# The order of additions and gathers on GpSimd's queue in a 64-expert mixture of experts

## What is computed

```python
x = hidden_states.reshape(-1, H)                       # T = 4096 rows of 512
probs = softmax(x @ gate_w)                            # E = 64 experts
w, idx = top_k(probs, 8)
...
buf = zeros((E, CAPACITY + 1, H)).at[e_flat, slot].set(x[tok])   # CAPACITY = 256 rows an expert
gu_e = einsum('ech,ehf->ecf', buf, expert_gate_up_w)
act = silu(gu_e[..., :I]) * gu_e[..., I:]
out_e = einsum('eci,eih->ech', act, expert_down_w)
y = out_e[e_flat, slot] * w_flat[:, None]              # summed over the 8 experts of a row
```

## Time and profile before

| | us |
|---|---|
| median of three runs | 2777.36 |
| the profiled execution's own time | 2763.05 |
| its span, first to last instruction | 2761.3 |
| TensorE busy (matmul) | 2557.5 (93% of the span) |
| TensorE weight loads busy | 1360.6 (49%) |
| VectorE busy | 1559.4 (56%) |
| ScalarE busy | 1353.8 (49%) |
| GpSimd busy | 1342.8 (49%), of it additions 240.9 and the experts' gathers 157.3 |
| mean granted TensorE clock | 0.97 |

### The profile page before, as it was taken

One profiled execution on the slowest core, in us unless ns is written; L12 is line 12 of the kernel. 1 busy time (PEld: TensorE's weight loads), 2 busy tenths in 40 slices (PEclk: granted clock), 3 DMA queues, 4 the chain that ended last, 5 costly groups with the idle time before them and its releaser, 6 DMA issues. The chain is left out here.

```text
span 2761.3 us, 43744 instructions
## 1 busy us (share of the span) xinstructions
PE 2557.5 (93%) x16510; PEld 1360.6 (49%) x16510; DVE 1559.4 (56%) x2474; ACT 1353.8 (49%) x3019; POOL 1342.8 (49%) x1043
## 2 busy tenths in 40 slices
PE   6888879999999899999999978887999999999999
PEld 4333334444444377777777634443444444444444
DVE  6899976555555255665655568775643332334222
ACT  4878874222222166666666468886433222232221
POOL 4777770665555546676666458886102211121111
PEclk9899999999999999999999989998999999999999
DMA  7899995222221399999999879998410111011000
GB/s 211 164 200 182 187 172 187 62 62 62 62 62 46 88 307 289 284 291 285 287 280 289 183 151 192 199 178 199 133 38 16 47 46 35 12 46 46 24 8 31
DMA packets 638576, 389.77 MB, mean 141 GB/s; under 512 B 472096, under 2 KB 575264, under 8 KB 634400
## 3 DMA queue, kind: packets, MB, share of 16 engines
q1 hardware_dynamic: 601504, 319.65, 45.6%
q0 software_dynamic: 36864, 67.34, 12.0%
HBM read 198.86 MB, written 75.89 MB: 99 GB/s over the span
## 5 line engine op out<-in xcount | busy, mean ns | idle before, releaser
L1765 POOL DMA_INDIRECT ids<-sh_tk,sh_su x256 | 269.2, 1052 | 243.0 <-PE sh_gu L55 69.5
L2714 POOL TENSOR_TENSOR fe_prodT<-fe_pp,fe_prodT 128x512 f16<-128x512 f32 x64 | 77.8, 1215 | 590.9 <-ACT fe_prodT L2499 590.9
L55 PE MATMUL ex_gu<-ex_xT,ex_h 128*128 128x256 f16 x3072 | 347.5, 273 | 2.8 <-issue 2.0
L2166 POOL DMA_INDIRECT xp<-ex_oo,ex_to x128 | 240.9, 1882 | 178.1 <-ACT ex_oo L2074 140.6
L55 PEld LDWEIGHTS ex_gu<-ex_xT,ex_h 128*128 128x128 f16 x3072 | 301.3, 98 | 51.9 <-issue 2.1
L1901 DVE SCALAR_TENSOR_TENSOR ex_h<-ring,ex_h 128x1024 f16<-128x1024 f32 x128 | 151.1, 1222 | 158.3 <-ACT ex_h L1891 158.3
L55 PE MATMUL at_g<-hm_zT,hm_w 128*128 128x512 f16 x768 | 187.0, 398 | 14.6 <-DMA hm_zT<-hm_zs 10.9
L2630 DVE SCALAR_TENSOR_TENSOR ring<-fe_g,fe_nf,ring 128x512 f32<-128x512 f32 x32 | 24.0, 751 | 293.1 <-PE fe_g L2415 293.1
L1875 POOL DMA_INDIRECT ex_xg<-zrows,ex_idxu x128 | 157.3, 1229 | 55.5 <-issue 31.1
L55 PE MATMUL sh_g<-sh_wdn,sh_actT 128*128 128x512 f16 x768 | 171.2, 382 | 10.3 <-issue 6.8
L55 PE MATMUL ex_o<-ex_h,ex_aT 128*128 128x512 f16 x768 | 177.9, 382 | 0.2 <-ACT ex_oo L2074 0.2
(11 more groups left out here) (367 smaller groups left out, 5375.7 us busy)
## 6 DMA issues: line engine op xcount, KB each, us to landing
ring<-L_ffn_expert_gate_up_w SPq DMA_DIRECT2D x128, 512.0 KB
ring<-L_ffn_expert_down_w SPq DMA_DIRECT2D x128, 256.0 KB
ring<-x SPq DMA_DIRECT2D x24, 1024.0 KB, 5.9
x<-ring SPq DMA_DIRECT2D x16, 1024.0 KB, 4.8
zrows<-hm_zs SPq DMA_DIRECT2D x32, 256.0 KB
xp<-ring SPq DMA_DIRECT2D x8, 1024.0 KB
out<-ring SPq DMA_DIRECT2D x8, 1024.0 KB, 4.3
ring<-xp SPq DMA_DIRECT2D x7, 1024.0 KB, 6.3
```

What stands on the lines that cost most here:

```text
L55: mm = nc.tensor.matmul(out, lhs(a, k), rhs(b, k), start=start and i == 0 and j == 0, stop=stop and i == n - 1 and j == 2)
L1765: e.indirect_dma_start(ids, bass.IndirectOffsetOnAxis(slotu[b % 2][:, t, j:j + 1], 0), pair[b % 2][:, t, j, :], None, bounds_check=SLOTS - ...
L2166: e.indirect_dma_start(dst, bass.IndirectOffsetOnAxis(to[:, n:n + 1], 0), o32[y % 2][:, t, :], None, bounds_check=T + SLOTS - 1, oob_is_er ...
L2714: e.tensor_tensor(prodT[:, 1, j, :], p32[q % 2][:, :], prodT[:, 0, j, :], ALU.subtract).then_inc(s["p_lo"], 1)
```

## The change

Only GpSimd's list changes. The four indirect DMAs of a round are the same ones with the same waits; their order becomes addition (y, 0), gather (y+5, 0), addition (y, 1), gather (y+5, 1).

```diff
-            for x in range(2, E + AHEAD):
+            def gather(x, t):
+                n = NS * x + t
                 if x < E:
-                    for n in range(NS * x, NS * x + NS):
-                        if n >= NG:
-                            e.wait_ge(s["x_mm"], n - NG + 1)
-                        X.gpsimd_rows(n, zrows)
-                if x >= AHEAD:
-                    y = x - AHEAD
-                    if y:
-                        e.wait_ge(added, 16 * NS * y)
-                    for t in range(NS):
-                        n = NS * y + t
-                        e.wait_ge(s["o_out"], n + 1)
-                        e.indirect_dma_start(dst, bass.IndirectOffsetOnAxis(to[:, n:n + 1], 0), o32[y % 2][:, t, :], None,
-                                             bounds_check=T + SLOTS - 1, oob_is_err=True, compute_op=ALU.add
-                                             ).then_inc(added, 16)
+                    if n >= NG:
+                        e.wait_ge(s["x_mm"], n - NG + 1)
+                    X.gpsimd_rows(n, zrows)
+
+            for x in range(2, AHEAD + 1):
+                for t in range(NS):
+                    gather(x, t)
+            for y in range(E):
+                if y:
+                    e.wait_ge(added, 16 * NS * y)
+                for t in range(NS):
+                    n = NS * y + t
+                    e.wait_ge(s["o_out"], n + 1)
+                    e.indirect_dma_start(dst, bass.IndirectOffsetOnAxis(to[:, n:n + 1], 0), o32[y % 2][:, t, :], None,
+                                         bounds_check=T + SLOTS - 1, oob_is_err=True, compute_op=ALU.add
+                                         ).then_inc(added, 16)
+                    gather(y + AHEAD + 1, t)
```

## The result

The new order took 3061.94 us (median of 5 runs, 3059.12 to 3063.17); the kernel before, run beside it, took 2775.11 us (5 runs, 2759.68 to 2780.97). The ratio is 1.1039, 95% interval 1.1019 to 1.1059. It is slower, as forecast, but by 287 us where 141 were forecast, and the time lies outside the range of 2830 to 2995. The profiled span is 3061.3 us, 300.0 more than before.

What follows compares the result with a forecast made beforehand. GpSimd's loop of landings was taken as the bound; its terms summed to 11.72 us a round, +140.9 us over 59 rounds, 2904 us profiled. With the runs' median 14.3 us higher, the forecast was 2918 us, range 2830 to 2995.

Steps and rivals of the forecast that it cites:

- The bound: Experts' stage: GpSimd's loop from landing to landing, 9.25 us a round, sets the pace; TensorE follows.
- The insertion: GpSimd, between the additions: gather 0 takes 1.62 us, addition 1 2.61; addition 1 ends 2.31 us later.
- Rival 1: GpSimd's round: gather 0 costs only 0.99 us, addition 1 1.57; +33 us, 2810; 8% together with its harsher form.
- harsher form: GpSimd's round: descriptor generation is small, so only the 0.30 us gap is added; +18 us, 2795; within the 8%.
- Covered work: ScalarE, VectorE and TensorE have 2.5 to 3 us of slack a round and cost nothing; rounds 59 to 63 stay.
- the tail: From the end of addition 1 on GpSimd to the next landing: taken as 4.5 us, the unknown term.
- the middle row: The tail of the profiled middle round before the change, 4.34 us, between ends of 3.62 and 6.26.
- argument against: On the tail: a longer round leaves the DMA engines, at 1.07 now, room, countering weights in flight; 4.5 us taken.
- Rival 2: Tail: weights get in addition 1's way, 6.26 us as in round 2; 13.48 us a round, +245 us, 3022; 8%.
- Rivals 3 and 4: Experts' rounds: faster, if TensorE's gather waits bound, 2750 (7%); unchanged, DMA engines alone setting the round, 2777 (5%).

Runs made afterwards that it cites:

- e1: c0 with a pause of three GpSimd memsets between the two additions of rounds 0 to 58, no gather between them; 3002.68 us.
- c1: Order after the change, with attention's DMA transposes replaced by plain copies and 1e-5 added inside one logarithm; 3042.74 us.
- e2: c1 with expert weight loads from expert 3 on cut to 8 of 256 columns, same number of packets; 2842.54 us.
- e4: c1 with full weights, SyncE issuing expert x's loads only once the additions up to expert x-7 have landed; 2856.09 us.
- c0: Order before the change, with attention's DMA transposes replaced by plain copies and 1e-5 added inside one logarithm; 2766.04 us.
- e5: c1 with the order gather 0, addition 0, addition 1, gather 1, all behind the landing; 2965.79 us.
- e7: c0 with SyncE's weight loads tied to the landing, by the same gate as in e4; 2809.71 us.
- e6: c0 with a pause of one GpSimd memset between the two additions; 2910.24 us.

## Why the prediction was right in its direction and wrong in its size

- **The bound** was read rightly. The loop of landings on GpSimd sets the stage: the page now names the landing as the releaser with 7 us, and the 291.6 us that 59 rounds gained are 97% of the 300.0 us that the span gained. TensorE's 93% and the DMA share of 1.07 were followers.
- **The insertion** was right: gather 0 and addition 1 both came out 0.05 us from the sum, through the reasoning about VectorE's splits. Only one direction of the blocking is borne out: GpSimd waits for a split, but VectorE's second split of L1901 starts while a gather or an addition is being made and is not later or longer for it (the two take 2.36 us together, before and after). Rival 1, the cheap insertion, fell with it: the gather took 1.66 us, not 0.99. Its harsher form by the Trainium skill, "DMA: Bandwidth & Descriptors", section "Anatomy of one DMA — SWDGE (gpsimd) path", where descriptor generation is small, fell too: the same row says 1.66 us, and gather 1, which meets no split, takes 0.98.
- **Covered work** behaved as said: ScalarE, VectorE and TensorE only wait longer, and rounds 59 to 63 took 42.3 us where they took 39.8. The whole delay reached the end: the first load behind the last landing moved from 1582.88 to 1881.65, 298.8 us.
- **The failed step is the tail.** The prediction wrote: "These two pull against each other. I take 4.5 us, close to the middle row." It measured 7.15 us on average. That is 2.65 us, and by 59 rounds 156 us; the prediction's 2904 us for the profiled execution and 156 make 3060, against the 3063.07 of the profiled execution after. The mechanism was named in the same paragraph ("with weights in flight ahead of it, as in round 2"), and then priced at 0.16 us above the middle row. e1 and c1 show what it costs, e2 and e4 that it goes with the weights, or with their place. In c1 the first packet of addition 1 comes 3.62 us behind its descriptors, in c0 0.83; that wait is what the 4.5 us had no room for.
- **Its argument against was the wrong one.** "The round is longer and the engines have room" averages over the round. The engines had room, but at the wrong time: they stood idle from 1206.8 to 1209.2, when nothing could be sent, and were full from 1213.9 to 1217.5, when addition 1 was ready. The length of the round gives nothing back, because the weights are tied to the landing as the additions are, and are asked for 4.6 us behind it in every order tried without a gate (before 1199.79 and 1204.42, after 1206.72 and 1211.35, e5 1199.78 and 1204.40).
- **Rival 2** was the right case, and was given 8%: "Rounds above 13 us would mean rival 2", and they are 14.27. Its price was short as well, with 6.26 us for the tail from round 2. In round 2 the down weights were still being handed over, from 1016.53 to 1021.77, when addition 1's descriptors were done at 1017.53; in the rounds here all loads lie ahead (the last is handed over at 1213.37). That difference between the row and the case was to be seen beforehand; that it explains the whole 0.9 us was not tested.
- **Rivals 3 and 4** fell with the direction.

What stays open is how the DMA engines choose. The windows show no sharing in small pieces: over the 3.6 us behind 1213.91, and over e4's 2.5 us from 1206, 923 and 845 weight packets pass and none of q0. The Trainium skill, "DMA: Bandwidth & Descriptors", section "Queues, rings and completion order", says that each engine takes its queues in turn and moves a whole packet of one before it goes to the next, and that such a packet holds some 9 to 17 descriptors as a rule and at most 64. If one packet of the profile is one such descriptor, which no run shows, a turn at its largest would be 1024 of them over 16 engines, by estimate, and the usual one 144 to 272. The medians of 698 to 1050 lie near the first and far above the second. So the rule can hold with turns near its upper end. Whether it is that, or the rows stand behind weights already handed further down, or the first packets of an addition wait for something else that weights delay, no run here tells. The step between 0.3 and 1.4 us behind the load's issue fits all three.

## What to carry to other kernels

Where transfers form a loop (issue, landing, next issue), price a delay by what the shared DMA engines will be doing at the new moment of issue: list the start of each large load as a distance from the loop's own event, and look whether the delayed transfer crosses one. Crossing it costs a step and not a proportion: here 1.15 us of delay cost 2.8 us a round. The size of the step was here not what was left of the burst, but the time that some 700 to 1050 of its packets took. A share averaged over the round, full or with room, says nothing about that. Where the burst can't be kept behind the transfer, it may be cheaper under time in which descriptors are being made anyway: e4 won with that, but e7, with less to cover it, lost.

## What the runs showed of the hardware that was not expected

- GpSimd's indirect transfers whose descriptors are ready after a 1.5 MB burst on SyncE's queue has begun got no packet, or next to none, for 2.95 to 3.62 us (c1, e1, e5, e6), against 0.58 us with 1/32 of the weights. About as many packets pass in that time wherever in the burst it begins. Once additions move they hold the larger part of the engines in turn: q0 90.0%, q1 10.7% in e4 from 1211.3, and 53.9 and 26.6% in the kernel after from 1217.5.
- TensorE's granted clock in the stage fell from 1.00 to 0.90, with 36% fewer products a microsecond (4138 in 784.00 us against 4107 in 497.80). In the stretch around the end of a wait of 3.47 us, which ends at 1207.52, the windows give 0.57:

```profile
1206.80:1209.20 2.40, 1.68 (x11) 1.13 (x12) 0.23 (x1) 2.40 (x4) 1.58 (x1) 0.57 0.01 3
```

  Its down products take 462 ns on average over the run now, where they took 382. No TensorE instruction is among the terms of the round above, so the loss isn't from there; a change that leans on TensorE's slack in such a loop would have to count it.
- The first instruction behind the landing starts sooner if it is a gather: 0.24 us (e5: landing at 1199.78 by ScalarE's copy, gather at 1200.02) in place of 0.78 for an addition. That it is the kind of transfer, and not a wait of the addition's own for the output copy, was not tested apart.
